# Exponentials' scores, then values, then the scores for the maxima in each attention step

## The reference

```
x = x + attention0(layernorm(x), ctx)   # 16 heads of 8, softmax over 512 keys
x = x + experts0(layernorm(x))          # 8 experts, hidden 512, the best one is taken
x = x + attention1(layernorm(x), ctx)   # 16 query heads on 8 key heads, inputs rounded to 8 bits
x = x + experts1(layernorm(x))          # 15 experts of 128 and a shared one, the best three
...
scores = einsum('bhqd,bhkd->bhqk', q, k) / sqrt(d)
out    = einsum('bhqk,bhkd->bhqd', softmax(scores), v)
```

## Time and profile before

| | |
|---|---|
| three runs | 287.5, 289.8, 290.75 us, median 289.8 us |
| span of the profiled execution | 281.9 us (its own time is not given beside it) |
| PE busy | 235.6 us, 84% |
| DVE busy | 177.7 us, 63% |
| ACT busy | 145.3 us, 52% |
| maxima, DVE L906 | 128 instructions of 686 ns |
| scores for the maxima, PE L1186 | 128 matmuls |
| scores for the exponentials, PE L1211 | 256 matmuls of 284 ns |
| values, PE L1226 | 512 matmuls |

### The profile page before, as it was taken

How to read it: one execution, slowest core, us unless ns; L and a number is a source line. 1 busy time by engine, 2 the same in 40 slices (tenths; PEclk the granted TensorE clock), 3 DMA queues, 4 the chain that set the end, 5 groups by cost and what they waited for, 6 DMA issues and landing times.

```text
span 281.9 us, 4880 instructions
## 1 busy us (share of the span) xinstructions
PE 235.6 (84%) x1685; PEld 152.1 (54%) x1700; DVE 177.7 (63%) x478; ACT 145.3 (52%) x336; POOL 54.4 (19%) x92
## 2 busy tenths in 40 slices
PE   2186345889999999999999999699699979889995
PEld 1035101344453545789988998343244424679985
DVE  5964797767656831421247137999577892589855
ACT  2026000657767686644435544366577678544542
POOL 8733982040402210100011300110000011021000
PEclk9999999799999999999999999959999999999999
DMA  6016327302270575800000110002100000000000
GB/s 158 0 60 226 150 72 162 110 4 80 74 205 22 149 190 137 215 5 2 1 0 0 58 56 2 1 0 58 56 4 0 3 0 0 3 0 0 21 1 20
DMA packets 20917, 16.26 MB, mean 58 GB/s; under 512 B 2085, under 2 KB 18989, under 8 KB 20797
## 3 DMA queue, kind: packets, MB, share of 16 engines
q1 hardware_dynamic: 20284, 15.76, 19.8%
q10 hardware_dynamic: 576, 0.13, 0.2%
q0 software_dynamic: 32, 0.07, 0.2%
HBM read 11.73 MB, written 4.19 MB: 56 GB/s over the span
## 4 chain that ended last, share of the span: by engine, by line
PE 65%; DVE 15%; ACT 7%; DMA 6%; issue 3%; SPq 2%; POOL 0%; DVEq 0%; ACTq 0%; another core or an unknown queue 0%
PE SB L1289 10%; PE OB L1226 8%; PE SA L1186 8%; DVE mx L906 7%; PE SB L1211 6%; PE OB L1302 5%; PE SB L1332 5%; PE SA L1302 5%; DMA Q<-nm 4%; PE SA L1342 4%; ACT prob L721 3%; DVE hn L871 3%; PE X L1154 2%; DVE qp L450 2%; PE X L1163 1%
## 5 line engine op out<-in xcount | busy, mean ns | idle before, releaser
L906 DVE TENSOR_REDUCE mx<-SA 128x1 bf16<-128x512 f32 x128 | 81.5, 686 | 20.0 <-PE SA L1186 15.9
L721 ACT ACTIVATE prob<-SB 128x512 f32<-128x512 f32 x128 | 69.4, 594 | 34.3 <-PE SB L1211 33.9
L1186 PE MATMUL SA<-K,Q 128*128 128x512 bf16 x113 | 41.5, 430 | 15.9 <-DVE mx L906 7.7
L1211 PE MATMUL SB<-Q,K 128*128 128x256 bf16 x256 | 41.6, 284 | 4.0 <-DMA Q<-nm 3.6
L782 ACT ACTIVATE prob<-SB,b1T 128x256 f32<-128x256 f32 x64 | 26.7, 471 | 28.5 <-PE SB L1289 28.4
L1226 PE MATMUL OB<-prob,V 128*32 128x256 f32 x512 | 39.7, 390 | 0.4 <-ACT oT L729 0.4
L1211 PEld LDWEIGHTS SB<-Q,K 128*128 128x128 bf16 x256 | 24.0, 101 | 24.9 <-ACT prob L721 6.8
L1289 PE MATMUL SB<-hT,w1s 128*128 128x256 f32 x128 | 33.3, 384 | 0.1
L1186 PEld LDWEIGHTS SA<-K,Q 128*128 128x128 bf16 x128 | 9.9, 102 | 35.6 <-DVE mx L906 23.9
L604 POOL TENSOR_SCALAR vareps<-mv 128x2 f32<-128x2 f32 x10 | 1.9, 192 | 137.2 <-DVE mv L850 137.2
L1289 PEld LDWEIGHTS SB<-hT,w1s 128*128 128x128 f32 x128 | 22.3, 190 | 3.6 <-ACT prob L782 0.7
(11 more groups left out here) (210 smaller groups left out, 282.4 us busy)
## 6 DMA issues: line engine op xcount, KB each, us to landing
w1s<-in_L_ffn_w_dram SPq DMA_DIRECT2D x8, 256.0 KB, 3.7
w2s<-in_L_ffn_w_dram SPq DMA_DIRECT2D x8, 256.0 KB, 4.4
K<-in_L_ffn_eW_dram SPq DMA_DIRECT2D x2, 960.0 KB, 6.5
K<-k_dram SPq DMA_DIRECT2D x8, 192.0 KB
Q<-q_dram SPq DMA_DIRECT2D x8, 192.0 KB
k_dram<-kp SPq DMA_DIRECT2D x2, 384.0 KB, 2.8
q_dram<-qp SPq DMA_DIRECT2D x4, 192.0 KB, 2.1
K<-k_dram SPq DMA_DIRECT2D x2, 384.0 KB
```

The lines of the kernel that those rows point to most:

```text
L721: act.activation(prob[:, g % 2, i, 2 * u:2 * u + 2, :].rearrange("p k q -> p (k q)"), SB[u][:, :], ACT.Exp).then_inc(s_exp, 1)
L906: dve.tensor_reduce(mx[:, g % 2, r, i:i + 1], SA[SCORE_BANK[n]][:, :], AX, ALU.max).then_inc(s_sa_max, 1)
L1186: pe.matmul(SA[SCORE_BANK[u]][:, :], Q[n][:, b, s, r * P:(r + 1) * P], K[n][:, b, key_group(n, s), :], start=True, stop=True).then_inc(s_s ...
L1211: last = pe.matmul(SB[u][:, k * NQ:(k + 1) * NQ], K[n][:, b, key_group(n, s), kt * P:(kt + 1) * P], Q[n][:, b, s, :], start=True, stop=True)
```

## The change

In `attention` the four lines that append S are moved from before E and V to behind them, still ahead of the extras. M(g+1) keeps its place at the head of the slot i = 1. No step is added or removed.

```
             for i in range(4):
                 if i == 1 and g0 <= g + 1 < g1:
                     steps.append(("max_rows", g + 1))
-                ahead = 4 * g + i + LEAD
-                if 4 * g0 <= ahead < 4 * g1:
-                    steps.append(("scores", ahead // 4, ahead % 4))
                 if g0 <= g < g1:
                     steps.append(("exp", g, i))
                 if g0 <= g - 1 < g1:
                     steps.append(("values", g - 1, i))
+                ahead = 4 * g + i + LEAD
+                if 4 * g0 <= ahead < 4 * g1:
+                    steps.append(("scores", ahead // 4, ahead % 4))
                 steps.extend(extra.get((g, i), []))
```

## The result

| | before | changed |
|---|---|---|
| median of four runs each | 288.65 us (286.08 to 290.75) | 302.0 us (300.32 to 303.14) |
| ratio | | 1.048, 95% interval 1.040 to 1.057 |
| span of the profiled execution | 281.9 us | 299.1 us |
| PE, DVE, ACT busy | 235.6, 177.7, 145.3 us | 241.3, 177.9, 144.3 us |
| M starts with PE idle ahead of it | 3.7 us in all | 12.8 us in all |

The kernel is slower, by 13.4 us between the medians; 300.5 was forecast. The ratios of this document leave out the upper runs of each kernel, the medians do not. The runs of before lie between 283.1 and 291.7 us in all of this document (37 runs, median 288.0), so a ratio of a few parts in a thousand has little weight, and I read causes from the traces.

What follows compares the result with a forecast made beforehand. PE bounds the steady attention, and each M without extras was to cost 1.10 us while PE waits for DVE's maxima. Layer 0's 5.6 and layer 1's 5.1 make +10.7 on 289.8: 300.5 us, range 296.5 to 304.5.

Steps and rivals of the forecast that it cites:

- M(1), seen at E(1,0): Start of layer 0: M(1)'s DMA is issued 1.7 to 2.0 us later but lands unchanged; 0 taken, bound +2.0.
- M(2), seen at E(1,1): Layer 0: w1_measure's reduction on DVE now follows the later maxima, delaying M(2) and the E after it, +1.65 us.
- M(3), M(4), M(5), M(6): Layer 0: PE pauses for DVE's maxima, 1.10 us each without extras, 0.75 behind four transposes, 0.31 behind vproj.
- M(7): Layer 0's last M: the pause for the maxima, partly filled by out_proj's 0.64 us, +0.70 us.
- head of layer 1, to E(10,1): Start of layer 1: PE's wait for M replaces its wait for the second batch's queries, net +0.8 us (-0.5 to +2.7).
- M(12), M(13): Layer 1, no extras on PE: PE pauses ahead of each M for DVE's maxima, +1.10 us each.
- M(14), M(15), to E(14,1): End of layer 1: M(14) +1.1 behind out_turn's DVE part, M(15) +1.0 from later first maxima, together +2.1 us.
- The cyclic argument: PE's slots: S E V becoming E V S is the same cycle started elsewhere; slots without M stay at 1.54 us.
- rival 2: PE's clock falls in new pauses: 302.5 to 305.5 us for one or two stretches, chance 0.24; 327 at all M, 0.03.
- The granted clock drops after the new pauses: Sign of being wrong: PE's granted clock falls after the pauses the change adds ahead of M; no size given.

Runs made afterwards that it cites:

- e12: The changed kernel measured once more, nothing altered: 300.4 us, ratio 1.058.
- e2: Changed kernel with scores behind exp and values in layer 0 only, layer 1 in the order of before: 294.0 us, ratio 1.037.
- e13: Repeat of e2, the change in layer 0 only: 293.3 us, ratio 1.029.
- e3: Changed kernel with scores behind exp and values in layer 1 only, layer 0 in the order of before: 296.4 us, ratio 1.042.
- e9: Kernel before, with o1's normalization moved from (13,2) to (14,1) and its followers one slot later each: 287.75 us, ratio 0.996.
- e10: Kernel before, with M(g+1) one step later, behind S(g+2,0), giving S, M, E, V: 289.0 us.
- e11: e10 with o1's normalization moved later as in e9: 288.2 us, ratio 1.014.
- e6: Changed kernel with o1's normalization moved from (13,2) to (14,1) and its followers one slot later each: 297.3 us, ratio 1.028.
- e1: Changed kernel with M(g+1) moved from the head of slot 1 to behind that slot's E and V: 290.9 us, ratio 1.021.
- e5: Changed kernel with 12 small extra matmuls on PE just ahead of its wait in each M: 301.7 us, ratio 1.045.
- e4: Changed kernel with LEAD 8 in place of 7, so S(g+1,3) comes a whole slot before M(g+1): 296.4 us, ratio 1.041.
- e8: Changed kernel with both M behind E and V (as e1) and the later o1 normalization (as e6): 292.0 us, ratio 1.012.

## Why the prediction was right, and where it was off

The time lay in the range and the mechanism is shown: M needs 1.78 us from its last scores, and E and V no longer fill them. The pauses at M(3) to M(6), M(12) and M(13) are right to 0.02 us; the rest of the sum was less good, and that the total came so near is in part luck (below). Term by term, from the start times of the same steps in both traces:

| term | forecast | measured |
|---|---|---|
| M(1), seen at E(1,0) | 0 | +0.2 |
| M(2), seen at E(1,1) | +1.65 | +1.76 |
| M(3), M(4), M(5), M(6) | 1.10, 0.75, 0.31, 1.10 | 1.10, 0.76, 0.31, 1.11 |
| M(7) | +0.70 | +1.14 |
| half clock behind M(2) | 0 | +1.65 (not there in e12, the same kernel) |
| head of layer 1, to E(10,1) | +0.8 | +1.5 |
| M(12), M(13) | 1.10 each | 1.12, 1.11 |
| M(14), M(15), to E(14,1) | +2.1 | +4.1 |
| half clock behind M(15) | 0 | +1.4 |
| whole | +10.7 | +17.2 |

(Small shifts between the terms make up the rest.)

**M(1).** That its transfer would land at the same time although issued later was the choice between 0 and 2.0. In this pair of traces it did: issued at 53.52 against 51.09, landed at 57.30 against 57.11. The Trainium skill ("DMA: Bandwidth & Descriptors", Queues, rings and completion order) says that each DMA engine consumes its ring's descriptors in order, and this pair agrees. But one pair does not show it. The landing, seen at E(1,0), varies by 4 us in one and the same kernel: 56.13 in e2 and 60.08 in its repeat e13. With the order of before in layer 0 (before, e3, e9, e10, e11) it is 57.6 us on average, with that of the change (changed, e2, e6, e13) 58.3, for an issue 1.7 us later. A difference of 0.7 is far inside this scatter, so the size of the term stays open; no run took the loads ahead of the transfer away.

**M(7)** was mis-sized by one S. No scores follow M(7), so E(6,0) to E(6,1) gained a whole S, 0.44 us, that before stood ahead of E(0,0) in a wait for DMA. The cyclic argument ("the same cycle started elsewhere") holds between two M and not at the ends.

**M(14), M(15)** is the step that failed in size. I followed DVE's queue and took the wait of E(14,0) for one on scores, which the change would take from its path. I did not follow ACT's queue: the exponentials of (13,3) stand behind a Square that waits for DVE's norm, and DVE's norm stands behind the maxima that now come 1.5 us later. The row was in the trace of before, where ACT already waited 1.74 us at that Square:

```profile
227.68 0.31 ACT L740 ACTIVATE junk<-hn 128x128 f32<-128x128 f32 x1 [1.74 <-DVE hn L869]
```

By parts, M(14) was forecast at +1.1 and came at +0.5, M(15) at +1.0 and came at +3.7, of which some 0.9 us are an estimate for half clock, from the spacing of its rows at 242.73 to 246.71. e1 (10.94 us with M's pause gone) and e6 (7.72 with the norm moved) show the wait.

**The head of layer 1** came out as described: turn at 198.96, 1.6 us later against M(8), the wait of 1.82 before S(12,0) gone, E(10,0) held 0.5 us by M(10)'s transfer. The 0.7 us above the forecast lie where E, V and qproj run at half clock (199 to 203).

**The clock**, rival 2, was given a chance of 0.24 for one or two stretches of 2 to 2.5 us each. Against the trace of before there are three new ones, behind M(2), at M(10) and behind M(15); the first costs 1.65 us, the last 1.4 beside its part in M(15). "The granted clock drops after the new pauses" was one of the signs of being wrong. After the usual pauses it does not drop: it is 1.00 in the steady stretches with 1.17 us idle at each M. The Trainium skill ("TensorE: Matmul & The Clock Gate", A second HAM failure mode) tells of a kernel whose short pauses between groups of matmuls made the clock swing. The usual pauses here do not, and e5 shows that filling them changes nothing.

What sets off the slow stretches stays open, and they do not belong to the change alone. The one behind M(2) is missing in the second trace of the changed kernel, e12, where M2 to M3 takes 8.05 us:

```profile
62.00:70.00 8.00, 7.42 (x65) 3.45 (x66) 5.19 (x15) 4.94 (x10) 3.72 (x9) 1.00 0.01 2
```

while e11, with S ahead of E and V, has one from 58 to 66. The one behind M(15) follows the wait for ACT ahead of E(14,0) in all six traces that have this wait (2.79 to 2.86 us: changed, e12, e3, e1, e4, e5). Of the eight without it, six stay at the full clock there, e6 among them, but e8 falls at 237 and e10 at 229. So the wait goes with the fall each time, and is not needed for it; that taking the wait away takes the fall away is not shown.

**The total.** The forecast of 300.5 is nearer to the medians than its terms deserve. Between medians the change costs 12.3 to 14.0 us, 1.6 to 3.3 more than the 10.7 of the terms. The base of 289.8, the median of three runs, was 1.8 us above the median of all, and that nearly made it good. The two profiled executions differ by more, 17.2 us, because that of before was a quick one. In later measurements time and span differ by 1.8 to 2.4 us (301.29 and 299.1 for the changed kernel), so a span of 281.9 belongs to a run of about 284, some 4 us under the median of before. Why it was quick is not shown. The recorded clock does not order the runs of before: 284.94 us with a mean of 0.939, 288.0 us with 0.970. I had added a difference from one execution to a median without asking whether they belong together.

## What to carry to other kernels

When a step waits for another engine's result, what counts is the work that stands between the producer's input and the waiting step in the program; moving a producer back behind independent work costs as much as that work, minus what was slack. The price of a late input is not only the wait at its consumer: follow each queue that the late work stands in, here ACT's exponentials behind a Square behind a norm behind maxima. And the rotation of the steps changed nothing in the slots without M of the steady stretches (1.54 us before and after), but everything that is pinned to a place in the loop (M here, and the first and last turn) has to be priced apart.

## What the runs showed of the hardware

- In the changed kernel's trace PE runs at half rate from 49.9 to 56 us (128x256 matmuls of E spaced 0.21 us, E taking 0.82 instead of 0.53), while the recorded granted clock of the stretch is 1.00:

```profile
49.80:56.50 6.70, 5.68 (x22) 2.62 (x22) 2.94 (x5) 3.63 (x7) 0.00 (x0) 1.00 0.31 105
```

  A second run of the same kernel records 0.50 for 49 to 57 us. So the recorded clock can miss a stretch, and the durations of the rows are the better witness.
- A small DVE operation can stand as long as a fill on GpSimd lasts. The cast of L450 took 5.41 us in the changed kernel, from 30.08 to 35.49, and 5.42 in the kernel before; GpSimd filled from 30.09 to 35.34. In e10, where the cast came 1.8 us earlier, it took 0.29 us, and instead an operation on 128x8 elements (L923) took 2.90, until the end of the longer fill. One kernel shows both: in e2 the cast (there L455) takes 0.29 us, in its repeat e13 7.11.

```profile
28.31 0.29 DVE L455 CAST qp<-qf 128x256 bf16<-128x256 f32 x1 [1.78 <-ACT qf L700]
```

```profile
28.66 7.11 DVE L455 CAST qp<-qf 128x256 bf16<-128x256 f32 x1 [2.00 <-ACT qf L700]
```

  M(0) then stands at 39.61 us in e2 and at 43.42 in e13, and the spans are 288.8 and 293.7 us. So this is one source of the spread between executions of one kernel. That the fill holds DVE is read from ends that coincide within 0.2 us; no run moved the fill.
